# Attention with two F32R parts a head, four heads in four row groups, and its batches written out one after another

## The reference, cut to what matters

```python
x = _layernorm(x + _L0_attn_ref(x, Wqkv, Wproj))      # causal
x = _layernorm(x + _L0_ffn_ref(x, ...))               # mixture of experts
x = _layernorm(x + _L1_attn_ref(x, Wq, Wk, Wv))       # full
x = _layernorm(x + _L1_ffn_ref(x, ...))               # dense
# attention, for each of 8 sequences:
q, k, v = heads(x @ Wq), heads(x @ Wk), heads(x @ Wv)  # 16 heads of 8
q = q * cos + rotate_half_interleaved(q) * sin         # k likewise
s = einsum('bhqd,bhkd->bhqk', q, k) / sqrt(8)          # causal: masked above the diagonal
y = einsum('bhqk,bhkd->bhqd', softmax(s), v)           # causal: y @ Wproj
```

## Time and profile before

| | |
|---|---|
| median of three runs | 1817.54 us |
| span of the profiled execution | 1812.5 us |
| TensorE busy | 1304.5 us, 72% |
| VectorE busy | 977.7 us, 54% |
| ScalarE busy | 856.7 us, 47% |
| GpSimd busy | 521.3 us, 29% |
| granted clock of TensorE, mean | 0.842 |
| first and last score product, causal attention | 72.9 and 624 us |
| first score product of the full attention | 925.5 us |

### The profile page before, as it was taken

The page is one execution under the profiler, slowest core; times in us unless marked ns, Lnnn a source line. Parts: engine busy times, 40 slices in busy tenths (PEclk is TensorE's granted clock), DMA queues, the critical chain, the costliest instruction groups (busy, mean ns, idle before and its releaser), DMA issues. The chain is left out here.

```text
span 1812.5 us, 26221 instructions
## 1 busy us (share of the span) xinstructions
PE 1304.5 (72%) x7355; PEld 675.7 (37%) x7355; DVE 977.7 (54%) x2508; ACT 856.7 (47%) x1575; POOL 521.3 (29%) x452
## 2 busy tenths in 40 slices
PE   1657648576595868784195876969678696899997
PEld 0323324233242355562021222213122122688885
DVE  2536446364374569345284855758467583235353
ACT  1235335253363574443143644647455475455553
POOL 6213133131241256473520201102021100345453
PEclk7669678697797969897567987989788799899999
DMA  4343241332422030342543314132240400000000
GB/s 72 38 55 35 33 54 29 51 37 31 54 38 30 2 119 0 93 82 61 58 88 38 39 22 53 20 47 29 31 49 16 49 2 7 12 12 15 20 12 18
DMA packets 84625, 70.22 MB, mean 39 GB/s; under 512 B 7628, under 2 KB 78476, under 8 KB 84508
## 3 DMA queue, kind: packets, MB, share of 16 engines
q1 hardware_dynamic: 80060, 64.78, 23.5%
q0 software_dynamic: 4176, 3.55, 1.4%
q10 hardware_dynamic: 272, 0.52, 0.1%
HBM read 17.84 MB, written 8.06 MB: 14 GB/s over the span
## 5 line engine op out<-in xcount | busy, mean ns | idle before, releaser
L671 DVE TENSOR_REDUCE a_mx<-a_ps_m 128x1 f32<-128x512 f32 (+3 forms) x864 | 547.2, 664 | 458.3 <-PE a_ps_m L535 254.2
L436 ACT ACTIVATE a_prob<-a_ps_s 128x512 f32<-128x512 f32 (+1 forms) x864 | 468.8, 576 | 505.7 <-PE a_ps_s L548 503.1
L548 PE MATMUL a_ps_s<-a_qst,a_kst 96*128 96x512 bf16 (+3 forms) x1024 | 349.3, 371 | 209.5 <-DMA a_qst<-a_mrow 172.0
L532 PE MATMUL a_ps_m<-a_kst,a_qst 72*128 72x512 bf16 (+3 forms) x1024 | 359.7, 376 | 152.5 <-DMA a_qst<-a_part_q 141.6
L548 PEld LDWEIGHTS a_ps_s<-a_qst,a_kst 96*128 96x128 bf16 x1024 | 93.1, 101 | 502.8 <-issue 246.6
L564 PE MATMUL a_ps_o<-a_prob,a_vst 128*32 128x512 f32 (+3 forms) x2048 | 245.4, 554 | 0.3 <-POOL a_prob L392 0.3
L392 POOL TENSOR_SCALAR_AFFINE_SELECT a_prob<-a_prob 128x512 f32<-128x512 f32 x128 | 81.2, 634 | 426.0 <-ACT a_prob L436 426.0
L532 PEld LDWEIGHTS a_ps_m<-a_kst,a_qst 72*128 72x128 bf16 x1024 | 107.5, 105 | 216.6 <-issue 172.2
L355 POOL TENSOR_TENSOR a_turned_k<-a_turned_k,sin_table 128x512 f32<-128x512 f32 x14 | 17.7, 1262 | 419.6 <-DVE a_rope_k L644 419.4
L1782 POOL TENSOR_TENSOR f_hid_lo<-f_gelu_h,f_hid_hi 128x512 fp32r<-128x512 f32 x64 | 83.1, 1298 | 101.0 <-ACT f_hid_hi L1745 101.0
L535 PE MATMUL a_ps_m<-mask,identb 128*128 128x128 bf16 x512 | 111.0, 240 | 0.0
(11 more groups left out here) (312 smaller groups left out, 1993.4 us busy)
## 6 DMA issues: line engine op xcount, KB each, us to landing
a_kst<-a_part_k SPq DMA_DIRECT2D x144, 128.0 KB
a_qst<-a_part_q SPq DMA_DIRECT2D x138, 128.0 KB
f_w<-in_L_ffn_W_dram SPq DMA_DIRECT2D x21, 256.0 KB, 3.6
a_xin<-in_L_attn_x_dram SPq DMA_DIRECT2D x8, 256.0 KB, 2.8
x_tiles<-in_L_attn_x_dram SPq DMA_DIRECT2D x8, 256.0 KB, 3.1
normed_rows_dram<-f_nrm SPq DMA_DIRECT2D x8, 256.0 KB, 2.3
f_hT_hi<-expert_sums_dram SPq DMA_DIRECT2D x4, 512.0 KB, 5.7
a_xin<-x_tiles SPq DMA_DIRECT2D x8, 256.0 KB, 2.4
```

What stands on the lines that cost most here:

```text
L436: act.activation(prob[j % RING][:, h:h + nu, 0:w], ps_s[(g * SU + u0 + slot) % SBANKS][:, 0:nu * w] .rearrange("p (h t) -> p h t", h=nu), ...
L532: last = pe.matmul(bank[:, v * w:v * w + w], qst[r][0:ROWS, h, P * i:P * i + P], kst[r][0:ROWS, h, 0:w], start=True, stop=not causal)
L548: last = pe.matmul(pbank[:, v * w:v * w + w], kst[r][:, h, P * j:P * j + P], qst[r][:, h, T - w:T], start=True, stop=True)
L671: dve.reduce_max(mx[:, g % 2, i, u * mh:u * mh + mh], ps_m[(unit + g * MU) % MBANKS][:, 0:mh * w] .rearrange("p (h t) -> p h t", h=mh), AX.X)\
```

## The change

Everything in `attention` is written anew; the expert layer and the dense layer are the same.

- q and k have two F32R parts each, `hi` and `lo`, and three products: hi x hi, hi x lo, lo x hi. That is 24 rows, with two more for the maximum. Each head of a group has a row group of its own, partitions 32 h to 32 h + 26, so a stack is 128 partitions x 4 groups x 512 values of four bytes. It takes 24 transfers of 8 partitions x 4 groups x 512 values; the row of maxima takes four transfers of 2 x 512 values.
- A group has `PH` phases: three in the causal attention, where the pieces of 384 and 128 keys share a bank, and four in the full one. In each phase every head has one score bank. The maxima run `LOOK` = PH + 3 phases ahead, and two heads stand in one tile of two banks, reduced in one operation.
- PSUM is one ring of three banks that ScalarE reads, one of two tiles of two banks that VectorE reads, and one bank for the weighted values.
- k and q are projected two batches ahead, in one tile; the rotation and the split into parts are four steps of two operations on GpSimd. The splitting of the maxima, into two parts, is on GpSimd too, as are the second residual and the last operation of the layer norm.
- The weighting of a phase is done in two halves, between score products.
- There is no loop over batches: all phases are written out, and x is loaded into its tiles once.

The core of the diff:

```diff
+def schedule(causal, wproj):
+    PH = 3 if causal else QT
+    LOOK = PH + 3
+    if causal:
+        chunks = [[(0, 0, T, 0)], [(1, P, T - P, 0), (3, 3 * P, P, T - P)], [(2, 2 * P, 2 * P, 0)]]
+        seen = [[(3, T, 0)], [(0, P, 0), (2, 3 * P, P)], [(1, 2 * P, 0)]]
...
+RING = 4
+LAG = 2
+SB, MB = 3, 2
+PAIRS = ((2, 3), (0, 1))
...
-        qst = [sbuf(f"qst{i}", [FULL, H, T], BF16) for i in range(2)]
-        kst = [sbuf(f"kst{i}", [FULL, H, T], BF16) for i in range(2)]
+        qst = [sbuf(f"qst{i}", [P, NG, T], F32R) for i in range(2)]
+        kst = [sbuf(f"kst{i}", [P, NG, T], F32R) for i in range(2)]
...
+                def stacks(b):
+                    sp.wait_ge(s_rope, ROPE_STEPS * (b + 1))
+                    if b >= 2:
+                        sp.wait_ge(s_filled, score_done((b - 1) * BATCH - 1))
+                    for i, dst, parts in ((0, kst[b % 2], (hi, hi, lo)), (1, qst[b % 2], (hi, lo, hi))):
+                        for slot, part in enumerate(parts):
+                            for hh in range(HG):
+                                row = VW * hh + SLOT_ROWS * slot
+                                sp.dma_start(dst[row:row + D, :, :].bitcast(F32),
+                                             part[VW * hh:VW * hh + VW, i, :].bitcast(F32)).then_inc(s_st[b % 2], 16)
...
+                for p in range(PHASES):
+                    b = batch_at(p, 0, 1)
+                    if b is not None:
+                        stacks(b)
+                    if turned_maxima(p) is not None:
+                        max_rows(turned_maxima(p))
...
-                with pe.Fori(0, B // 2 - 1) as it:
-                    batch(2 * it + 1, 1)
-                    batch(2 * it + 2, 0)
...
+                for p in range(LAST):
...
+                    if live:
+                        scores(p, 0)
+                    if old is not None:
+                        weigh(old, 0)
+                    if live:
+                        scores(p, 1)
+                    if p + LOOK < PHASES:
+                        maxima(p + LOOK, 0)
+                    if live:
+                        scores(p, 2)
+                    if old is not None:
+                        weigh(old, 1)
+                    if live:
+                        scores(p, 3)
...
+                    for i, w, c0 in seen[ph]:
+                        ins = dve.reduce_max(mx[:, n % 2, i, h:h + 2], tile[:, :, c0:c0 + w], AX.X)
...
+                for p in range(LAST + SCALE_PHASES):
+                    if turned_maxima(p) is not None:
+                        split_max(turned_maxima(p))
+                    if causal and p < PHASES:
+                        hide(p)
+                    for step in range(4):
+                        b = batch_at(p, F_ROPE + step, 2)
+                        if b is not None:
+                            rope_step(pool, b, step)
```

More of the change, by code:

```diff
@@ L20 @@
 PARTS = 3
[L21 to L24 removed]
+SWAP = [i ^ NG for i in range(NG * D)]
 VW = 32
@@ new lines, in _ @@
+                sp.wait_ge(s_sign, 1)
+                for st in kst:
+                    for hh in range(HG):
+                        row = VW * hh + KEYS
+                        sp.dma_start(st[row:row + 2, :, :].bitcast(F32),
+                                     sign[:, :].unsqueeze(1).to_broadcast([2, NG, T])).then_inc(s_ones, 16)
+                stacks(0)
+                if x_dram is not None:
+                    for b in range(2, B):
+                        sp.dma_start(xb(b), x_dram[b]).then_inc(s_x[b], 16)
@@ new lines, in weigh @@
+                def weigh(p, half):
+                    n, ph = divmod(p, PH)
+                    b, g = divmod(n, NG)
+                    if half == 0:
+                        if causal:
+                            pe.wait_ge(s_masked, p + 1)
+                        else:
+                            pe.wait_ge(s_taken, score_done(p))
+                        if ph == 0 and n >= 1:
+                            pe.wait_ge(s_oT, n)
+                    parts = halves[ph][half]
+                    for j, q0, w, c0 in parts:
+                        for hh in range(HG):
+                            last = pe.matmul(ps_o[VW * hh:VW * hh + VW, q0:q0 + w], vst[b % 2][:, j, HG * g + hh, :],
+                                             prob[p % RING][:, hh, c0:c0 + w], start=(ph == 0 and half == 0),
+                                             stop=(ph == PH - 1), skip_group_check=True)
+                    if parts and (half == 1 or not halves[ph][1]):
+                        last.then_inc(s_pv, 1)
@@ new lines, in scales @@
+                def scales(p, half):
+                    for k in range(SCALE_PHASES):
+                        b = batch_at(p - k // 2, F_LN, -1)
+                        if b is not None and k % 2 == half:
+                            scale_phase(b, k)
+                for st in vst:
+                    dve.memset(st[:, :, :, D + 1:VW], 0.0).then_inc(s_vinit, 1)
+                    dve.memset(st[:, :, :, D:D + 1], 1.0).then_inc(s_vinit, 1)
+                turn_heads(0)
+                for step in range(4):
+                    rope_step(dve, 0, step)
```

889 lines of the change are left out of this document (391 added, 498 removed).

## The result

The changed kernel takes 2042.7 us (median of 4 runs, 2036.2 to 2047.0), the kernel before 1816.9 us: a ratio of 1.123, 95% interval 1.118 to 1.129. It is 12% slower, and lies far outside the forecast range.

What follows compares the result with a forecast made beforehand. Transfers into eight partitions were taken to set the batch, with TensorE waiting on them. Full batches saved 35 us, causal 17, first, last and starts the rest: -70 from 1817.5 to 1747 us, range 1620 to 1850.

Steps and rivals of the forecast that it cites:

- The clock behind the stand: TensorE in each batch, after waiting for the row of maxima: lower clock for a while, costing 4 us.
- my sum: Main case over all batches: full 71.6 us, causal 70.7 us, together -70 us, so 1747 us; chance 0.45.
- 12 x 3.3 + 4: Full batch after its stacks arrive: twelve phases of 3.3 us left, plus 4 us for the low clock.
- The phase, 8 x 0.22 + 2 x 0.57: TensorE, full attention: eight products and two half weightings make 2.90 us, with turning and projections 3.3 us.
- nearly none: Gain from neighbouring row groups overlapping on TensorE, at most 0.3 us twice a phase; the overlap rival: 1667 us, chance 0.18.
- my third rival: TensorE: changes between 32-row and 128-row products empty the array; at 0.2 us each 1853 us, slower; chance 0.17.
- the causal jobs: Turning x, o and y and the projections on TensorE, causal attention: 2.0 us a group in the forecast.
- VectorE's reduction of two heads: VectorE's maximum over two heads in one operation: 1.13 us each, twice a full phase.
- The stacks, 28 us: DMA of each batch's 24 transfers of 64 KB into eight rows: 1.57 MB at 59 GB/s, 28 us.
- The rival with fast stacks: Stack transfers bound by packet count, not bytes: 15 us a batch, about 1500 us in all; chance 0.12.
- the 54 GB/s of the prediction's estimate: Stack DMA rate: eight rows reach two ports, estimated as 54 GB/s from the page's 435 GB/s over 16.
- The row of maxima behind all stacks: SyncE's queue: the row of maxima follows all 24 stack transfers, so TensorE waits once a batch, 15 to 20 us.

Runs made afterwards that it cites:

- the stretches: Blocks of products alone on TensorE, put ahead of the changed kernel's first attention; its row of ten steps took 2.46 us at full clock, 4.32 at the lower.
- before_k24: The kernel before, with score and maxima products cut to 24 rows, order, BF16 and transfers kept: 2187.9 us, ratio 1.203.
- wide: The changed kernel with scores and maxima over all 128 rows, k's stack kept once per head with zeros in other heads' rows: 1879.0 us, ratio 1.033.
- max_act2: The changed kernel with the row of maxima sent from ScalarE's queue, ScalarE's copy of the weighted sums ahead of it: 1940.0 us, ratio 1.066.
- quad64: The changed kernel with scores and maxima over 64 rows, ordered two scores, two maxima, half a weighting, everything on SyncE's queue: 1753.1 us, ratio 0.964.
- quad64_pool: As quad64, but GpSimd issues q's stacks and SyncE sends the row of maxima between pieces of k's: 1559.8 us, ratio 0.858.

## Why the prediction was wrong

**The clock behind the stand, "+ 4 (low clock after the stand)": the step that failed.** I took a stretch of 12.9 us at the lower level behind each stand from a trace in which products had 72 and 96 rows, and carried it over to products of 24 and 26. The other number of rows stood in the change itself, and I asked only what it does to the columns. In the full batch from 1188.3 us the stand ends after 28.3 us, as in my sum; the rest, to 1284.0 us, takes 67.4 us, where I had 12 x 3.3 + 4 = 43.6. Nearly all of the difference is the clock, by an estimate from the stretches: the same row of steps takes 2.46 us at the full clock and 4.32 at the lower, and 12 x 1.86 is 22 of the 24 us. That the rows bring the level down is shown by before_k24 (rows alone, 1.203, clock 0.50) and wide (rows back, 164 us less), and that the stands do not by max_act2. What brings the level down and holds it inside the kernel is less simple than "few rows", and stays open: the same rounds keep either level when they run unbroken, and do not keep the upper one in the kernel.

**The phase, 8 x 0.22 + 2 x 0.57.** Its columns were right, its form not. Row groups do overlap (0.01 us between starts), which I had put aside as "nearly none" and given 0.18 as a rival. At the full clock that is worth 0.9 us a phase: 2.46 against 3.38 us for the round with 128 rows. The latter is above the sum of its columns: eight products of 0.23 and two half weightings of 0.42 make 2.66, and four changes the other 0.72, 0.18 us each. I had 0.1 for a change, and my third rival decided "from 0.17 us upwards"; in the stretches the price is there, but overlap pays for it. The rival's time, 1853 us, would have been nearest to the result, by another mechanism; that would have been luck. Two sizes were small besides: the causal jobs, 10.5 us a batch, are 2.6 us a group and not the 2.0 of the sum, and VectorE's reduction of two heads took 1.23 us and not 1.13.

**The stacks, 28 us.** Right: 24 transfers were issued from 1188.9 us, and the row of maxima behind them released TensorE at 1216.6 us, at 60 GB/s. The rival with fast stacks is refuted: a third of the packets, 768 in place of 2304, moved their bytes no faster. The rate lies a tenth above the 54 GB/s of the prediction's estimate, before and after, so that two ports are what bounds it is not shown.

**The row of maxima behind all stacks.** It was right in kind and number, once a batch, 14 in all; the mean is 12.9 us (causal) and 8.7 us (full) where I said 15 to 20, since slower phases cover more. Its worth is 103 us in the changed kernel (max_act2), and more where phases are short: quad64 to quad64_pool is 193 us, with q's stacks on another queue as part of that edit.

**The sum.** In the six inner full batches 6 x (95.2 - 71.6) = 142 us, in the causal ones 6 x (82.8 - 70.7) = 73 us: 215 of the 296 us between forecast and result, all of it in phases. Much of the rest lies in the outer batches, by the same clock: the last full one takes 75.4 us from its first to its last score, where the kernel before took 48.7. VectorE and ScalarE, forecast at 2.8 and 2.3 us a phase, never came into play until the order changed; there VectorE binds, at 2.6.

## What to carry to other kernels

Before packing small products into row groups, look at how many of them truly run side by side at each step, and order them so that none runs alone; then read the granted clock of the stretch, since a busy TensorE at 0.50 looks the same in the busy row. A short transfer that others wait for must not stand behind long ones: pace the long ones in pieces around it, and give it to a queue whose engine has time. A gain on one engine lengthens the next stand when a transfer of fixed length sets the batch, so take both edits together: the order was worth 314 us alone, the queues another 193 us at 64 rows. And count what an edit adds at the start of a stage: with the zeros of wide the first scores of its two attentions came 19 and 27 us later.

## What the hardware showed that I had not expected

The granted clock has a memory: the same 40 rounds stay at 1.00 for 90 us or at 0.50 for 160 us, by what ran before them. BF16 products over 75 rows, one at a time, keep either level too. The kernel before, with 72 and 96 rows, therefore comes up behind its stands probably by its weightings, which raised the clock when they ran alone; this was not tried in it. Without weightings, rounds of three products side by side and one alone fell to 0.50 even behind full products. Four row groups of 24 rows in turn took 55 ns a product of 512 columns (9 us over 164 records). Four issues of 4 KB transfers held ScalarE's queue for 2.41 us, as long as four exponentials.
